# A graph network on one core: the two relational layers' dense loops and the second layer's tables in one block, with that layer's scale taken from a bound

## The chip, the cores and the metric

The kernel runs on 1 core of one Trainium2 chip. The metric is the device time of one execution in microseconds (us), and the median over several runs is compared. The core has five engines that run side by side and meet only at semaphores: TensorE (PE, matrix products), VectorE (DVE), ScalarE (ACT), GpSimd (POOL) and SyncE (SP, which here issues most of the DMAs).

## The reference, cut to what matters

A graph of 3125 nodes with 96 features and 103125 edges (source, destination, one of 8 relation types) goes through four residual steps, each followed by a layer norm: ten propagation steps, an attention over the edges, two relational layers, and two layers that sum over neighbours. The change is in the third step:

```
for l in range(2):                       # L2
    xb = h.reshape(N, B, S)              # 8 blocks of 12 features
    transformed = einsum('nbi,rbio->rnbo', xb, weights[l]).reshape(R, N, D)
    msg = transformed[etype, src] * (1 / in_degree)[dst]
    agg = segment_sum(msg, dst)
    h_new = agg + h @ loop_w[l] + bias[l]
    h = relu(h_new) if l == 0 else h_new
x = layernorm(x + h)
```

The input h of the first of the two layers is a layer norm's output; that of the second is the first's result through relu. weights[l] has 8 relations x 8 blocks x 12 x 12 values.

## The kernel before, in words

Nodes lie in NT = 25 tiles of 128. The kernel is a series of blocks. In a block each engine has its own written-out list of instructions; at a block's end all engines meet, and a block's PSUM tensors are freed and others allocated. The attention stage (main block from line 1263) comes first, then the relational layers (lines 1399 to 2050), then the last step (from 2060). For each relational layer (`for layer in range(2)`, line 1458) there are two blocks.

**Tables.** For each node tile t, PE multiplies the transposed features `ht` (97 rows, the last one all 1) with `bd`, the block-diagonal weights of all 8 relations beside loop_w and bias: one product of 480 columns and one of 384 into two PSUM banks, in f32 (`table_products`, L1494 and L1495). ACT takes loop_w's part into `hn` (L1499) and the relations' part, scaled to a safe power of two, as the f16 high half into `tab` (L1500, `high_out`). DVE writes the f16 low half, the scaled product less the high half (L1504, `low_out`). SP stores each tile of `tab` in memory (`store_table`, L1483). Three bank pairs are used in turn, so the product of tile t waits for the low half of tile t - 3.

**Dense loop.** For each of the TD = 19 first destination tiles and each of 8 relations DVE makes a mask of edge counts out of packed words in `code` (`relation_mask`, L1474; four mask buffers in turn, released by `s_free`), and PE adds 25 products mask x tab into one PSUM bank (`tile`, L1888). That is 3800 products per layer. The edges into the last GT = 6 tiles are done by gathering: ACT makes one-hot matrices (L1948 to L1956), POOL gathers 12 x 128 rows of the table from memory (L1864), each gather released by a tick of PE (`s_pace`), and PE multiplies them (L1896). Edges that the packed words can't hold go through `irregular_edges` (L1921, L1928) after tile 0. DVE reduces each finished bank (L1985) and adds it to `goal` (L1990), which is `hn` in the first layer and `x` in the second. At a loop's end DVE adds the last gathered tile and then the last dense tile.

**What sets the scale.** In the first layer, before any table, the scale is taken from `btop`: the weights' largest value times SUB = 12 times `LN_BOUND`, the largest value a layer norm of 96 features can give. `btop` comes from `bmost`, a [128, 2] tile that DVE fills in the attention stage (L1385, L1387) and POOL reduces over the partitions (L1282). In the second layer DVE takes the largest weight (L1509) and the largest value in all of `hn` (L1765). PE turns the two columns (L1748), DVE reduces them (L1514, L1515), PE spreads them over the partitions (L1751), and DVE works out the scale and the scaled degrees (L1768, L1769, L344 to L347, L1519 to L1521) and releases `s_sc`, for which PE waits before its first table product. The 25 transposes of `hn` (`rows_turned`, L1742), with ACT's relu copy of five at a time (L1782), stand around these steps.

The masks of the dense loop's first relations are made while the tables are made: four in the first layer, and in the second one ahead of DVE's low halves and one after each of the tiles 8, 14 and 20 (L1774 to L1776). SP loads the words of the first three tiles at the start of the block (L1723). The weights of the second layer are loaded into `bd` during the first layer's dense loop (`load_relations(e, 1, s_load)`).

Of the kernel before, what the change touches and what calls it, by code (L numbers as in the profile page):

```python
# [16 lines left out]
P = 128  # L17
N = 3125
D = 96
# [58 lines left out]
def gnn_kernel(nc, a, out):  # L78

    with ExitStack() as top:  # L80
# [1044 lines left out]
        bmost = sb("bmost", [P, 2], F32)  # L1125
        btop = sb("btop", [P, 2], F32)
# [3 lines left out]
        with ExitStack() as ph:  # L1130
# [115 lines left out]
            with ExitStack() as main:  # L1246
# [18 lines left out]
                with nc.Block() as block:  # L1265
                    @block.gpsimd
                    def _(e):
# [13 lines left out]
                        e.wait_ge(s_bd, 2)  # L1281
                        e.partition_all_reduce(btop[:], bmost[:], P, bass.bass_isa.ReduceOp.max).then_inc(s_bd, 1)  # L1282
                        e.wait_ge(s_bd, 3)
# [81 lines left out]
                    def _(e):  # L1365
# [33 lines left out]
        with ExitStack() as ph:  # L1399
            sb = new_sb(ph)  # L1400
            ht = flat
            most = sb("l2_most", [P, 2], F32)
            both = sb("both", [2, 3], F32)
            ones = sb("ones", [2, P], F32)
            st2 = sb("l2_maxima", [P, 2], F32)
# [52 lines left out]
            for layer in range(2):  # L1458
# [3 lines left out]
                s_in = [sem(nm + f"in{k}") for k in range(SLOTS)]  # L1462
                s_mask = sem(nm + "mask")

                def load_code(e, t):
                    e.dma_start(code[:, t % SLOTS, :, :, :].rearrange("p q s d -> p (q s d)"),
                                code_dram[t, :, :, :, :].rearrange("p q s d -> p (q s d)")).then_inc(s_in[t % SLOTS], 16)

                def relation_mask(e, t, r):

                    up = 10 - 2 * r
                    turned = mask[:, r % MR, :, :].rearrange("p s d -> p (s d)").bitcast(I32)
                    words = code[:, t % SLOTS, :, :, :].rearrange("p q s d -> p (q s d)").bitcast(I32)
                    e.tensor_scalar(turned.rearrange("p (s q d) -> p s q d", q=NQ, d=DQ // 2),  # L1474
                                    words.rearrange("p (q s d) -> p s q d", q=NQ, d=DQ // 2), abs(up), 0x0C000C00,
                                    ALU.logical_shift_left if up >= 0 else ALU.logical_shift_right,
                                    ALU.bitwise_and).then_inc(s_mask, 1)
# [11 lines left out]
                s_dve, s_most, s_mt, s_diag, s_mp, s_sc = (sem(nm + k) for k in ("tdve", "most", "most_t", "diag", "most_p", "sc"))  # L1489
# [16 lines left out]

                def weights_largest(e):
                    e.wait_ge(s_load, 16 * LOADS)
                    e.tensor_reduce(most[0:D, 0:1], bd[0:D, :, 0:HW2], mybir.AxisListType.XY, ALU.max,  # L1509
                                    apply_absolute_value=True).then_inc(s_most, 1)  # L1510

                def maxima_over_partitions(c, e, most_t):
                    e.wait_ge(s_mt, 1)
                    c(e.tensor_reduce(both[:, 0:1], most_t, AX_X, ALU.max))  # L1514
                    e.tensor_scalar(both[:, 1:3], ident[0:2, 0:2], both[:, 0:1], None, ALU.mult).then_inc(s_diag, 1)  # L1515
# [7 lines left out]
                if layer == 0:  # L1523
                    with ExitStack() as ph:
# [12 lines left out]
                        s_att, s_read, s_mean, s_sq, s_var, s_std, s_x, s_one = (  # L1537
                            sem("ln1_" + k) for k in ("att", "read", "mean", "sq", "var", "std", "x", "one"))
# [981 lines left out]
```

## Time and profile before

| | |
|---|---|
| median of 3 runs | 2339.51 us (2338.59 to 2343.16) |
| profiled execution, own time | 2347.8 us |
| its span, first to last instruction | 2346.1 us |
| PE / DVE / ACT / POOL busy in the span | 2155.6 / 1825.4 / 1164.0 / 881.5 us |
| mean granted TensorE clock | 0.965 |
| first layer's tables and dense loop | about 1369 to 1780 us |
| second layer's tables and dense loop | about 1782 to 2171 us |

The profile comes from one execution. Busy times are sums of an engine's instructions; the span is the time from the first to the last instruction, and what the execution took more than it lies around it. The granted clock is the share of full speed (2.4 GHz) that the chip grants TensorE; it is 1.00 or 0.50 at any moment, and a value between is a mean over a stretch.

### The profile page before, as it was taken

To read this page: it belongs to the slowest core of one execution; us is meant where nothing else is said; L and a number is where in the kernel's file an instruction comes from. 1 tells how busy PE (TensorE), PEld (TensorE's weight loads), DVE (VectorE), ACT (ScalarE), POOL (GpSimd) and SP (SyncE) were. 2 spreads that over 40 slices of the span, in tenths; PEclk is the share of its full clock that TensorE was granted. 3 is DMA by queue.
4 is the path that set the end of the run, shared out by engine and by line. 5 is a ranking of instruction groups with operands and counts; after the bars stand their busy time and mean duration, and the time that the engine had idled before them with its cause. 6 is when DMAs were issued, how large, how long until landed. Compare 5 with 4: busy or idle time off the path is not lost. (4 is left out here: it accounts for less than half of the span.)

```text
span 2346.1 us, 63182 instructions
## 1 busy us (share of the span) xinstructions
PE 2155.6 (92%) x22505; PEld 1791.3 (76%) x22505; DVE 1825.4 (78%) x2687; ACT 1164.0 (50%) x2788; POOL 881.5 (38%) x1062
## 2 busy tenths in 40 slices
PE   2888888899999999789999968999999999999897
PEld 2888887899999999522222235999996899999787
DVE  8999999655555666579999976988886788887446
ACT  1888888332332332379999955222313432230323
POOL 2444444000000000068888823555551455555000
PEclk8999999899999999789999979999999999999799
DMA  2444444210000010332222234232224323222800
GB/s 67 157 169 168 173 177 176 76 39 30 31 29 31 29 44 2 102 84 56 58 58 57 58 116 147 75 87 76 75 60 149 119 74 89 74 74 44 352 5 22
DMA packets 94801, 205.77 MB, mean 88 GB/s; under 512 B 21718, under 2 KB 61270, under 8 KB 94450
## 3 DMA queue, kind: packets, MB, share of 16 engines
q1 hardware_dynamic: 81458, 182.46, 22.3%
q0 software_dynamic: 13120, 20.18, 4.4%
q8 instruction: 159, 2.61, 0.5%
q14 instruction: 64, 0.52, 0.1%
HBM read 116.99 MB, written 84.76 MB: 86 GB/s over the span
## 5 line engine op out<-in xcount | busy, mean ns | idle before, releaser
L1888 PE MATMUL l_bank<-tab,mask 128*128 128x192 f16 x7600 | 636.8, 247 | 8.8 <-PEq L1719 3.5
L1888 PEld LDWEIGHTS l_bank<-tab,mask 128*128 128x128 f16 x7600 | 629.4, 98 | 11.9 <-issue 11.3
L1474 DVE TENSOR_SCALAR mask<-code 128x1600 int32<-128x1600 int32 x304 | 544.4, 1816 | 95.3 <-PE l_bank L1888 70.9
L1864 POOL DMA_INDIRECT ggot<-table_dram,gidx x408 | 386.8, 948 | 265.4 <-PE l_bank L1888 206.3
L1371 DVE TENSOR_TENSOR pr<-ex,count_copy 128x1568 f32<-128x1568 f32 x200 | 350.5, 1786 | 25.6 <-POOL ex L1270 13.8
L1361 ACT ACTIVATE ex<-score_pair,poss 128x784 f32<-128x784 f32 x400 | 344.2, 910 | 30.2 <-PE score_pair L1309 18.9
L1270 POOL TENSOR_SCALAR ex<-ex 128x1568 f32<-128x1568 f32 x200 | 298.5, 1493 | 78.5 <-ACT ex L1361 71.2
L906 PE MATMUL sums<-onehots,ct 128*128 128x192 f16 x3125 | 264.4, 248 | 11.2 <-issue 4.8
L906 PEld LDWEIGHTS sums<-onehots,ct 128*128 128x128 f16 x3125 | 261.5, 99 | 13.9 <-issue 7.5
L906 PE MATMUL sums<-u,ct 128*128 128x192 f16 x3125 | 259.1, 246 | 0.0
L906 PEld LDWEIGHTS sums<-u,ct 128*128 128x128 f16 x3125 | 258.0, 98 | 0.0
L459 POOL COPY wqk<-edges 128x6 f32 x400 | 163.7, 440 | 226.0 <-ACT wqk L643 113.3
L965 DVE TENSOR_REDUCE onehots<-sums 128x96 f32<-128x192 f32 x250 | 89.2, 357 | 176.2 <-PE sums L906 170.0
L1948 ACT ACTIVATE gidx<-rowidx 128x12 int32 x34 | 7.2, 211 | 428.0 <-PE l_bank L1896 387.4
L1309 PE MATMUL score_pair<-qa,ka 96*128 96x392 f16 x800 | 205.6, 340 | 3.6 <-ACT ex L1361 2.2
L1309 PEld LDWEIGHTS score_pair<-qa,ka 96*128 96x128 f16 x800 | 47.5, 98 | 184.8 <-ACT ex L1361 176.3
L1325 PE MATMUL att_acc<-pr,v 128*32 128x392 f32 x1600 | 176.5, 513 | 5.8 <-DVE pr L1371 5.8
L570 PE MATMUL counts<-onehots,flat 128*128 128x200 f16 x1200 | 143.1, 254 | 39.4 <-DVE onehots L491 35.5
L883 POOL PARTITION_ALL_REDUCE wtop<-wmax x1 | 0.4, 374 | 432.2 <-DVE wmax L996 432.2
L491 DVE TENSOR_TENSOR onehots<-iota,wqk 128x1200 f16<-128x1200 f16 x200 | 155.4, 777 | 0.0
L575 PE MATMUL codes<-onehots 128*128 128x200 f16 x1200 | 140.3, 251 | 0.0
L1042 ACT ACTIVATE u<-onehots,rdeg 128x96 f16<-128x96 f32 x125 | 46.7, 374 | 186.3 <-DVE onehots L965 186.2
(342 smaller groups left out, 2939.0 us busy)
## 6 DMA issues: line engine op xcount, KB each, us to landing
code<-code_dram SPq DMA_DIRECT2D x38, 800.0 KB
code_dram<-flat SPq DMA_DIRECT2D x100, 200.0 KB, 1.9
ct_dram<-ct SPq DMA_DIRECT2D x25, 800.0 KB, 3.6
c_dram<-flat SPq DMA_DIRECT2D x25, 800.0 KB, 3.4
ct_again<-ct_dram SPq DMA_DIRECT2D x25, 800.0 KB, 17.3
cring<-c_dram SPq DMA_DIRECT2D x200, 98.0 KB, 2.0
table_dram<-tab SPq DMA_DIRECT2D x50, 384.0 KB, 2.3
flat<-code_dram SPq DMA_DIRECT2D x19, 800.0 KB, 4.4
```

Source lines behind the costliest of these rows:

```text
L459: ins = e.tensor_copy(rec[:, w % RECS, h * GRP:(h + 1) * GRP, :], edge_rec[:, bass.ds(chunks[h], GRP), :])
L491: e.tensor_tensor(hot[:, k, :, :, :], iota[:], each(col[:, k, :], WC), ALU.is_equal).then_inc(s_hot, 1)
L570: e.matmul(counts[:, b, h * WC:(h + 1) * WC], chunk_of(srchot, k, j), chunk_of(hot, k, j), start=False, stop=False, skip_group_check=True)
L906: mm = e.matmul(sums[t % RS][:, 0:2 * D], ct[:, t, s, :], u[par][:, s, :, :].rearrange("p k d -> p (k d)"), start=(s == 0), stop=(s == NT ...
L1270: ins = e.tensor_scalar(ex[n % UR][:], ex[n % UR][:], EXP_HIGH, EXP_LOW, ALU.min, ALU.max)
L1309: mm = e.matmul(pair_ps[k][:, h, 0:QC], ka[0:D, k * HP2 + h, j * P:(j + 1) * P], qa[0:D, k * HP2 + h, b * QC:(b + 1) * QC], start=True, st ...
L1325: mm = e.matmul(acc[h * HW:(h + 1) * HW, b % 2, 0:QC], v[:, j, h, :], pr[n % UR][:, h, :], start=(j == 0), stop=(j == NT - 1), skip_group_ ...
L1361: e.activation(ex[n % UR][:, k * HP2:(k + 1) * HP2, :], pair_ps[k][:, :, 0:QC], ACT.Exp, scale=poss[:]).then_inc(s_ex[k], 1)
L1371: e.tensor_tensor(pr[n % UR][:], ex[n % UR][:], c_ps[n % 2][:, 0:QC].unsqueeze(1).to_broadcast([P, H, QC]), ALU.mult).then_inc(s_pr, 1)
L1474: e.tensor_scalar(turned.rearrange("p (s q d) -> p s q d", q=NQ, d=DQ // 2), words.rearrange("p (q s d) -> p s q d", q=NQ, d=DQ // 2), abs ...
L1864: e.indirect_dma_start(ggot[:, k, j, :], None, table_dram[:, :], bass.IndirectOffsetOnAxis(ap=gidx[:, k, j:j + 1], axis=0)).then_inc(s_ggo ...
L1888: mm = e.matmul(acc[k][:, 0:2 * D], mask[:, r % MR, s, :], tab[:, s, r, :], start=(r == 0 and s == 0), stop=(r == R - 1 and s == NT - 1))
```

## The change

One block now holds the first layer's dense loop, the second layer's tables and its dense loop (`stages`); the first layer's tables keep their block. One PSUM tensor `l2_bank` serves all three, and semaphores that both layers use (`s_in`, `s_mask`, `s_free`, `s_acc`, `s_gsum`) count on over the layers (`n = layer * TD + t`). The second layer's scale is worked out from a bound on the first layer's result: (the first layer's bound on the rows x 12 x the largest weight, plus (D + 1) times the largest of loop_w and bias) x 12 x the second layer's largest weight. For that the attention stage loads the second layer's weights once more and takes two more maxima.

```diff
-        bmost = sb("bmost", [P, 2], F32)
-        btop = sb("btop", [P, 2], F32)
+        bmost = sb("bmost", [P, 4], F32)
+        btop = sb("btop", [P, 4], F32)
+        W1_ROWS, W1_COLS = R * NB, SUB * SUB
+        w1_raw = spare[0:W1_ROWS, 4 * (HW2 + D):4 * (HW2 + D) + 2 * W1_COLS].bitcast(F32)
...  (attention stage, POOL: e.wait_ge(s_bd, 2) -> 4 and 3 -> 5 around partition_all_reduce)
...  (attention stage, SP)
                                 load_relations(e, 0, s_bd_in)
+                                e.dma_start(w1_raw, a["weights"][1].rearrange("r g i o -> (r g) (i o)")).then_inc(s_bd_in, 16)
...  (attention stage, DVE)
-                                e.wait_ge(s_bd_in, 16 * LOADS)
+                                e.wait_ge(s_bd_in, 16 * (LOADS + 1))
+                                e.tensor_reduce(bmost[0:D + 1, 2:3], bd[0:D + 1, 0, HW2:], AX_X, ALU.max,
+                                                apply_absolute_value=True).then_inc(s_bd, 1)
+                                e.tensor_reduce(bmost[0:W1_ROWS, 3:4], w1_raw, AX_X, ALU.max,
+                                                apply_absolute_value=True).then_inc(s_bd, 1)
...  (second layer's tables: weights_largest, maxima_over_partitions and what they use are gone)
+                def tables(bank):
+                    table = [bank[:, b:b + 2, :] for b in (6, 1, 4)]
+                    turned = [five(bank[:, b:b + 2, :]) for b in (4, 1)]
+                    def sync(e):
+                        for t in range(SLOTS):
+                            n = layer * TD + t
+                            e.wait_ge(s_mask, (n - SLOTS + 1) * R)
+                            load_code(e, n)
+                        for t in range(NT):
+                            e.wait_ge(s_lo, t + 1)
+                            store_table(e, t)
...  (gpsimd: the additions to x as before)
+                    def tensor(e):
+                        def rows_turned(g):
+                            if g == 0:
+                                e.wait_ge(s_acc, TD - 1)
+                            if g >= 2:
+                                e.wait_ge(s_ht, g - 1)
+                            e.wait_ge(s_goal, max(ADDED.index(t) + 1 for t in range(5 * g, 5 * g + 5)))
...  (five transposes)
+                        for g in range(G):
+                            rows_turned(g)
+                        e.wait_ge(s_load, 16 * LOADS)
+                        e.wait_ge(s_gsum, GT)
+                        for t in range(NT):
+                            e.wait_ge(s_ht, (1, 4, G)[t] if t < 3 else G)
+                            if t >= 3:
+                                e.wait_ge(s_lo, t - 2)
+                            table_products(e, table[t % 3], t)
+                    def vector(e):
+                        c = Chain(e, s_dve)
+                        c(e.tensor_scalar(power[:], btop[:, 2:3], float(D + 1), None, ALU.mult))
+                        c(e.tensor_scalar(scale[:], btop[:, 0:1], float(SUB) * LN_BOUND, None, ALU.mult))
+                        c(e.tensor_tensor(power[:], power[:], scale[:], ALU.add))
+                        c(e.tensor_scalar(power[:], power[:], btop[:, 3:4], float(SUB), ALU.mult, ALU.mult))
+                        degrees_scaled(c, e)
+                        e.wait_ge(s_free, layer * TD * R + MR)
+                        relation_mask(e, layer * TD, MR - 1)
+                        for t in range(NT):
+                            low_out(e, table[t % 3], t)
+                        e.wait_ge(s_xadd, G)
...  (scalar: as before)
...  (dense loop, PE)
                             for r in range(R):
+                                e.wait_ge(s_mask, n * R + (r + 1))
                                 for s in range(NT):
+                                    if layer and t == 0 and r == 0 and (s == 0 or s >= NT - 2):
+                                        e.wait_ge(s_lo, max(NT - 2, s + 1))
...  (dense loop, DVE: add_to_goal now releases s_goal; the loop's end)
+                        if layer == 0:
+                            code_there(e, TD)
+                            for r in range(MR - 1):
+                                masked(TD, r)
+                        summed(TD - 1)
                         for g, j in groups_behind(TD - 1) + groups_behind(TD):
                             if j == SLOTS - 1:
                                 gathered(g)
-                            summed(TD - 1)
...
+            main0 = layer_of(0)
+            tables1, main1 = layer_of(1)
+            with nc.psum_tensor("l2_bank", [P, 8, 512], F32) as l2_bank:
+                stages = [main0(l2_bank), tables1(l2_bank), main1(l2_bank)]
+                with nc.Block() as block:
...  (each engine runs its part of the three stages in turn)
```

`s_goal` counts the sums added to `goal`, and `ADDED` lists in which order they come, so that each group of five transposes waits only for its own tiles. In the words of before: `rows_turned(g)` stood in another block than the additions. Two memsets of POOL at the start of the first layer's tables (`most`, `ones`) are gone.

## Rows read from the trace of the kernel before

**Rows 1.** The page, engine totals, and its costliest group of DVE.

```profile
PE 2155.6 (92%) x22505; PEld 1791.3 (76%) x22505; DVE 1825.4 (78%) x2687; ACT 1164.0 (50%) x2788; POOL 881.5 (38%) x1062
...
L1474 DVE TENSOR_SCALAR mask<-code 128x1600 int32<-128x1600 int32 x304 | 544.4, 1816 | 95.3 <-PE l_bank L1888 70.9
```

**Rows 2.** Busy time by stretch: the second tables' start, the second dense loop.

```profile
core 0: us, PE busy (x) PEld busy (x) DVE busy (x) ACT busy (x) POOL busy (x), PEclk, DMA share, GB/s
...
1782.00:1800.00 18.00, 16.63 (x50) 9.66 (x50) 11.04 (x17) 8.23 (x15) 0.00 (x0) 0.72 0.50 192
...
1947.00:2160.00 213.00, 212.77 (x2579) 212.60 (x2578) 184.03 (x133) 52.51 (x138) 125.55 (x135) 1.00 0.27 71
```

**Rows 3.** Timeline: start, duration, engine, line, count, [idle before]; first loop to tables.

```profile
1777.78 1.15 PE L1896 MATMUL l_bank<-ggot,goh 128*128 128x192 f16 x12
1778.97 0.36 DVE L1985 TENSOR_REDUCE part<-l_bank 128x96 f32<-128x192 f32 x1 [6.97 <-PE l_bank L1896]
...
1779.99 0.32 DVE L1990 SCALAR_TENSOR_TENSOR hn<-part,rdk,hn 128x96 f32<-128x96 f32 x1
...
1781.84 3.41 PE L1742 MATMUL ht_bank<-ident,hn 128*96 128x128 f32 x15 [2.91 <-PEq L1834]
...
1785.29 0.70 ACT L1782 ACTIVATE flat<-ht_bank 96x640 f32<-96x640 f32 x1 [0.37 <-PE ht_bank L1742]
...
1786.91 0.21 DVE L1769 TENSOR_SCALAR tpower<-l_maxima 128x1 f32<-128x1 f32 x1
...
1788.26 0.17 DVE L1521 COPY rdk<-rds 128x6 f32<-128x6 f32 x1
...
1788.49 1.94 PE L1494 MATMUL ht_bank<-spare,flat 97*128 97x480 f32 x2 [1.14 <-DVE rdk L1521]
```

**Rows 4.** Timeline of the second tables: after a mask, and two undisturbed tiles.

```profile
1819.48 1.07 PE L1494 MATMUL ht_bank<-spare,flat 97*128 97x480 f32 x2 [0.48 <-DVE tab L1504]
...
1822.48 0.97 PE L1494 MATMUL ht_bank<-spare,flat 97*128 97x480 f32 x2
...
1823.93 0.97 PE L1494 MATMUL ht_bank<-spare,flat 97*128 97x480 f32 x2
```

**Rows 5.** Timeline: the second tables' end and the dense loop's start.

```profile
1829.84 0.81 PE L1495 MATMUL ht_bank<-spare,flat 97*128 97x384 f32 x2
...
1831.76 1.02 DVE L1504 SCALAR_TENSOR_TENSOR tab<-ht_bank,tscale,tab 128x768 f16<-128x768 f32 x1 [1.03 <-ACT tab L1500]
1831.87 1.19 POOL L1733 TENSOR_TENSOR x<-x,hn 128x480 f32<-128x480 f32 x1 [6.79 <-ACT tab L1500]
...
1834.11 11.13 PE L1888 MATMUL l_bank<-tab,mask 128*128 128x192 f16 x100 [3.46 <-PEq L1719]
...
1835.85 0.18 POOL L1851 COPY idx<-rowidx 128x1 int32 x1 [2.79 <-POOLq L362]
```

**Rows 6.** Stretches of PE alone: length, busy, granted clock, DMA share, GB/s.

```profile
1400.00:1409.00 9.00, 5.83 (x19) 1.00 0.37 151
...
1788.40:1795.00 6.60, 6.51 (x9) 0.51 0.17 69
1796.00:1830.70 34.70, 33.20 (x90) 1.00 0.59 238
1834.00:1840.00 6.00, 5.89 (x39) 0.52 0.17 57
```

**Rows 7.** Timeline of the first layer: five warm transposes; the dense loop's start.

```profile
1396.33 0.71 PE L1574 MATMUL ln_bank<-ident,x 128*96 128x128 f32 x5
...
1442.29 7.25 PE L1888 MATMUL l_bank<-tab,mask 128*128 128x192 f16 x86 [3.44 <-PEq L1539]
```

**Rows 8.** Timeline of the attention stage: weight loads, first maximum, POOL's reduction.

```profile
1049.62 0.27 SPq L356 DMA_DIRECT2D spare<-in_bias  x1
...
1051.91 0.51 PE L1317 MATMUL count_copy<-cring,exact 128*128 128x392 f16 x1 [7.32 <-DMA cring<-c_dram]
...
1142.65 0.94 DVE L1385 TENSOR_REDUCE bmost<-spare 96x1 f32<-96x768 f32 x1
...
1367.66 0.37 POOL L1282 PARTITION_ALL_REDUCE btop<-bmost  x1 [6.01 <-issue]
```

More of the change, by code:

```diff
@@ L1456, in gnn_kernel, with load_code @@
             s_load = sem("l2_load")
-            for layer in range(2):
+            s_in = [sem(f"l2_in{k}") for k in range(SLOTS)]
+            s_mask, s_free, s_acc, s_gsum, s_goal = (sem("l2_" + k) for k in ("mask", "free", "acc", "gsum", "goal"))
+            assert R % MR == 0
+            def load_code(e, n):
+                e.dma_start(code[:, n % SLOTS, :, :, :].rearrange("p q s d -> p (q s d)"),
+                            code_dram[n % TD, :, :, :, :].rearrange("p q s d -> p (q s d)")).then_inc(s_in[n % SLOTS], 16)
@@ new lines, in gnn_kernel @@
+            fixed = lambda g: SLOTS - 1 if g < GT - 1 else 1
+            GROUPS = [(g, k) for g in range(GT) for k in list(range(fixed(g))) + [SLOTS - 1]]
+            LAND = 60
+            DENSE = TD * R * NT
+            begun = [4 + i * (DENSE - LAND - 4) // (len(GROUPS) * GG) for i in range(len(GROUPS) * GG)]
+            ticks = {n - 1 - (n % NT == 0) for n in begun}
+            behind = [min(TD - 1, (begun[GG * n + GG - 1] + LAND - 1) // (R * NT)) for n in range(len(GROUPS))]
+            due = [sum(b <= t for b in behind) for t in range(TD)] + [len(GROUPS)]
@@ new lines, in gnn_kernel, with layer_of @@
+            assert len(ticks) == len(begun) < 1 << 16 and due[TD - 1] == len(GROUPS)
+            groups_behind = lambda t: GROUPS[due[t - 1] if t else 0:due[t]]
+            ADDED = [0]
+            for t in range(2, TD):
+                ADDED += [t - 1] + [g + TD for g, k in groups_behind(t - 1) if k == SLOTS - 1]
+            ADDED += [TD - 1] + [g + TD for g, k in groups_behind(TD - 1) + groups_behind(TD) if k == SLOTS - 1]
+            assert sorted(ADDED) == list(range(NT))
+            def layer_of(layer):
@@ new lines, in vector, with _ @@
+                        summed(TD - 1)
+                        for g, j in groups_behind(TD - 1) + groups_behind(TD):
+                            if j == SLOTS - 1:
+                                gathered(g)
+                    return sync, gpsimd, tensor, vector, scalar
+                return (tables, main) if layer else main
+            main0 = layer_of(0)
[3 more added lines that the diff above has]
+                with nc.Block() as block:
+                    @block.sync
+                    def _(e):
+                        for sync, _, _, _, _ in stages:
+                            sync(e)
+                    @block.gpsimd
+                    def _(e):
+                        for _, gpsimd, _, _, _ in stages:
+                            gpsimd(e)
+                    @block.tensor
+                    def _(e):
+                        for _, _, tensor, _, _ in stages:
+                            tensor(e)
+                    @block.vector
+                    def _(e):
+                        for _, _, _, vector, _ in stages:
+                            vector(e)
+                    @block.scalar
+                    def _(e):
+                        for _, _, _, _, scalar in stages:
+                            scalar(e)
```

515 lines of the change are left out of this document (214 added, 301 removed).

## The prediction

> **What bounds the kernel now.** I read the engine totals first: TensorE (PE) is busy for 92% of the span, far above VectorE (DVE) at 78%; the costliest group of DVE is the relation masks, 1.82 us each [rows 1]. That alone says nothing about this change, so the second view was the stage table. In the dense loop of the second relational layer PE is busy 212.77 of 213 us at full clock; in the stretch in which that layer's tables begin it has the granted clock 0.72 [rows 2]. So the loops are bound by PE, and what can be won lies at their borders. The third view, the timeline of the border, shows what stands there. The last product of layer 0 ends at 1778.93, DVE adds until 1780.31, the block ends, and PE starts again at 1781.84. Then come 25 transposes, with the search for the rows' maximum between them, and the scale chain, whose last instruction is at 1788.26. The first table product starts at 1788.49, 9.56 us after the last useful product [rows 3]. At the other end the last table product ends at 1830.65 and the first dense product starts at 1834.11: 3.46 us for ScalarE's (ACT's) copy, DVE's 1.02 us copy and a block border [rows 5]. The fourth view is the granted clock. It was 0.51 over the first 6.6 us of the tables and 0.52 over the first 6 us of the dense loop, both 1.2 GHz for nearly all of it, and 1.00 in between [rows 6].
>
> **Border one, loop 0 to tables.** Removed: the block border, the reduction over all of hn, the transposed maxima and their spreading product. PE's next instructions are the transposes. Groups 0 to 3 need sums that DVE has added by then, because the last dense tile's sum now goes before the gathered one, while PE still does its 12 gathered products (1.15 us). Five warm transposes took 0.71 us [rows 7] and ACT's copy of five takes 0.70 [rows 3]. With two buffers, counted from 1778.93: the first copy ends at 1.45 and frees group 2, which ends at 2.2; the second ends at 2.2 and frees group 3; the third ends at 2.95 and frees group 4, which ends at 3.65. The first product follows at once, since it needs only the first copy. 9.56 - 3.65 = 5.9 us saved. Bounds: nothing less than 25 transposes back to back (some 3.0 us), and if all ran cold, as those five did whose copy of 0.70 us came after 0.37 idle, 5 x 1.07, with the first wait some 5.5 us; so 4.1 to 6.6.
>
> The scale chain is no longer ahead of the products, only ahead of ACT's first copy. It has ten small operations; the seven from 1786.91 to 1788.43 took 1.5 us [rows 3], so ten take 2.1. They start when DVE's last addition ends, some 0.75 us after the last product, and end at 2.9 us. ACT's transposed copies end at 4.4 and the first table product at 5.1, so the chain costs nothing; without that cover it would cost its excess over 5.1. Behind it on DVE stands the fourth mask (1.82 us), over at 4.8, before DVE's first table copy can start at 6.2. The other three masks move into layer 0's last dense tile, into DVE's 6.97 us without work [rows 3]. They take 5.5 us; each waits for a mask buffer that PE frees every 2.05 us (25 products of 82 ns), and the last is over just before PE is. If they overran, the tile's sum would come late by that much, and group 3 of the transposes has 2.2 us to spare.
>
> **The tables.** Now 1788.49 to 1830.65 = 42.16 us. A warm tile takes 1.45 us (1822.48 to 1823.93), so 25 take 36.25. The rest is two things: half clock at the start, and three masks of 1.8 us between DVE's copies, after which PE waited for a buffer (0.48 us idle, and a tile 0.75 us longer) [rows 4, 6]. 3 x 0.75 = 2.2; the clock has the other 3.6. The change moves the masks away, and if PE stays warm through the transposes the clock's part goes too: 5.9 us, bounds 2.2 (clock falls again) to 5.9. Late next would be ACT: 0.90 and part of 0.25 us for each tile, 1.04 against 1.45, so PE remains the bound.
>
> **Border two, tables to loop 1.** The dense loop now waits for DVE's copy number 22, and its last two products of the first relation for copies 23 and 24. A copy ends 2.13 us after its product (1830.65 to 1832.78) [rows 5], so copy 22 ends 0.8 us before the last product does. Copy 24 ends 2.13 after; 24 dense products take 2.0. 3.46 - 0.2 = 3.2 us saved, bounds 1.3 (the loop waits for copy 24) to 3.4. The first 100 dense products took 11.13 us [rows 5]; in layer 0, where the clock had not fallen although the pause before was as long, 86 took 7.25 [rows 7], so 100 take 8.43. Saved: 2.7, bounds 0 and 2.8, since the same pause has cost nothing once.
>
> Waits added here: DVE waits for GpSimd's (POOL's) last addition to x, over 2.4 us after the last product [rows 5]; behind it stands the mask that needs relation 0 finished, at 2.3 us; nothing is lost, as PE wants it at 8.4. The gathers still need all tables in memory: POOL's first index copy came 3.07 us after DVE's last copy [rows 5], now 5.2 us into the loop instead of 1.7. The 3.5 us of delay fall into a first tile of 16.5 us, at whose end their first data are used. On SP the three code loads go ahead of the table stores; their masks' condition is met at 1772, so nothing queues behind them.
>
> **End of loop 1.** The last sum of 0.36 us and its addition of 0.32 [rows 3] go under the gathered products: 0.7 us saved.
>
> **Costs in the attention stage.** SP issues one more load of weights in the place where PE already waits 7.32 us for counts queued behind such loads; an issue takes 0.27 [rows 8]: 0.3 us, bounds 0 and 0.6. DVE does two more reductions, over 96 and 144 elements where 768 took 0.94 us [rows 8]: by size 0.3, with a start 0.45, bounds 0 and 1.9. ACT and DVE are both nearly full here, so I take 0.3. The reduction over partitions gets four columns for two, and POOL ends this block last: it took 0.37 with 6.01 us of issue ahead [rows 8]; nearest is nothing to 0.37, I take 0.1, and 6.4 if all of it grew with the columns.
>
> **Sum.** 5.9 + 5.9 + 3.2 + 2.7 + 0.7 - 0.7 = 17.7 us. The profiled execution took 2347.8 us (span 2346.1 and 1.7 around it), so 2330.1. It was 0.35% above the median, 2339.51, from which the same sum gives 2321.8; I say 2322.
>
> **Rivals.** (1) The clock falls in the transposes or the first tables. For it: it fell there before, when PE transposed with pauses, and after the pause in which the scale was awaited. Against: in layer 0's tables it stayed 1.00 over 9 us in which PE was busy 5.83 [rows 6], and transposes and tables now are denser than that. Price: a fall cost 3.6 us at the tables: 2325.5. The Trainium skill speaks for this rival ("TensorE: Matmul & The Clock Gate", A second HAM failure mode): PE that idles briefly but often while it cycles through PSUM banks has its clock go down and up again. By it the saving would lack that same fall; the 9 us at 1.00 disagree with it, the 0.51 agrees.
>
> (2) The change does only part of what it says: a wait returns at a border (copy 24 before the loop, 2.1 us, with it a cold start, 2.7), or the attention costs are at their upper ends (8.9 for 0.7). 5 to 9 us less: 2327 to 2331; with both, 2335, no change.
>
> (3) Slower. The two dense loops and the tables become one stretch of some 710 us in which PE never rests. If the granted clock falls inside it, each microsecond at half speed costs half a microsecond: it takes 45 us at 1.2 GHz to turn 17.7 us gained into 4.7 lost, 2344 and more. For it: nothing so long is in the trace. Against: 213 us at 1.00 with PE busy throughout [rows 2].
>
> **How the numbers follow.** Forecast 55%, own range 2318.5 to 2324.5; rival 1 22%; rival 2 17%, of which 6% end within 0.2%; rival 3 6%. A measurement of this kernel tells about 0.2%, 4.7 us, from no change. So faster 0.88, same 0.06, slower 0.06. The range goes from 2317 to 2331, with rival 1 and most of rival 2 in it.
>
> **What would show it.** Right: PE idle under 1 us between layer 0's last gathered product and the first transpose; first table product 3.4 to 4.2 us after it; table products 1.45 us apart from the first on, with clock 1.00; less than 0.4 us between the last table product and the first dense one; the first 100 dense products in about 8.4 us; a pause near 7.6 us at the counts in the attention stage. Wrong: a clock of 0.5 in any of these stretches, table tiles at 2.9 us, PE waiting in loop 1 for gathered rows after the first tiles, or POOL's reduction ending more than 0.5 us later after the last clip than before.

## The result, and the profile after

The changed kernel takes 2327.55 us (median of 4 runs, 2326.39 to 2328.19), the kernel before 2341.34 beside it (4 runs, 2338.59 to 2344.73). The ratio is 0.994, with a 95% interval of 0.9926 to 0.9954: 13.8 us less, between 10.8 and 17.3. I had said 2322. The time is 5.5 us above that: 1.8 of them lie in the kernel before, whose median was 2339.51 when I took it and 2341.34 beside the changed one, and 3.9 in the saving, 13.8 us for 17.7. It lies outside the 2318.5 to 2324.5 that I had put on the forecast and where I had put rival 2, and yet neither condition of that rival came: between the two loops every stretch became what the forecast said.

The page of after, engine totals and DVE's costliest group, against [rows 1]:

```profile
PE 2143.6 (92%) x22502; PEld 1784.1 (77%) x22502; DVE 1827.9 (79%) x2687; ACT 1164.4 (50%) x2788; POOL 884.8 (38%) x1060
...
L1477 DVE TENSOR_SCALAR mask<-code 128x1600 int32<-128x1600 int32 x304 | 548.7, 1817 | 81.4 <-PE l_bank L1876 80.4
```

PE has the same work but for three small products, and its busy time is 12.0 us shorter, of 21.0 between the two spans: over half of that difference is nearly the same work done in less time, with the mean granted clock at 0.972 for 0.965. The totals show no more. The timeline of after at border one (start, duration, engine, line, [idle before]) answers [rows 3]:

```profile
1774.56 1.15 PE L1884 MATMUL l_bank<-ggot,goh 128*128 128x192 f16 x12
...
1775.55 1.26 PE L1752 MATMUL l_bank<-ident,hn 128*96 128x128 f32 x10
...
1777.05 1.35 PE L1752 MATMUL l_bank<-ident,hn 128*96 128x128 f32 x10 [0.24 <-ACT flat L1781]
...
1778.30 0.17 DVE L1536 COPY rdk<-rds 128x6 f32<-128x6 f32 x1
1778.38 1.81 DVE L1477 TENSOR_SCALAR mask<-code 128x1600 int32<-128x1600 int32 x1
...
1778.59 0.75 PE L1752 MATMUL l_bank<-ident,hn 128*96 128x128 f32 x5 [0.19 <-ACT flat L1781]
...
1779.18 0.97 PE L1519 MATMUL l_bank<-spare,flat 97*128 97x480 f32 x2
...
1780.63 0.97 PE L1519 MATMUL l_bank<-spare,flat 97*128 97x480 f32 x2
```

The last gathered product ends at 1775.71 and the first table product starts at 1779.18, 3.47 us later, 9.56 before. The transposes wait only for ACT's copies, 0.24 and 0.19 us. The scale chain ends at 1778.47, long before ACT's first table copy, and the fourth mask runs behind it. The tables are 1.45 us apart from the first on.

Busy time of PE by stretch in after, against [rows 2, 6]: length, busy, granted clock, DMA share, GB/s.

```profile
1775.00:1779.00 4.00, 3.56 (x33) 1.00 0.00 0
1779.00:1785.00 6.00, 6.00 (x21) 1.00 0.17 66
1785.00:1816.00 31.00, 31.00 (x92) 1.00 0.69 271
1816.00:1822.00 6.00, 5.79 (x71) 1.00 0.46 178
...
1830.00:2150.00 320.00, 318.73 (x3877) 1.00 0.28 71
```

The clock is 2.4 GHz (1.00) in all of them; nowhere between the two loops does it fall. So the rival that it falls in the transposes or tables did not come, nor the one that it falls in the long stretch without rest. The Trainium skill ("TensorE: Matmul & The Clock Gate", A second HAM failure mode) has the clock go down and up where PE idles briefly and often between groups of products; the two pauses of 0.24 and 0.19 us here did nothing of the kind.

The timeline of after at border two, against [rows 5]:

```profile
1814.79 0.81 PE L1520 MATMUL l_bank<-spare,flat 97*128 97x384 f32 x2
...
1815.43 2.15 PE L1876 MATMUL l_bank<-tab,mask 128*128 128x192 f16 x24
...
1816.71 1.02 DVE L1529 SCALAR_TENSOR_TENSOR tab<-l_bank,tscale,tab 128x768 f16<-128x768 f32 x1 [0.43 <-ACT tab L1525]
...
1817.79 8.42 PE L1876 MATMUL l_bank<-tab,mask 128*128 128x192 f16 x100 [0.21 <-DVE tab L1529]
...
1820.86 0.18 POOL L1836 COPY idx<-rowidx 128x1 int32 x1 [2.84 <-POOLq L362]
```

The dense loop starts as the last table product ends, its 24 products cover DVE's last copy but for 0.21 us, and 100 more take 8.42 us, where I had said 8.43. POOL's first index copy is 5.4 us into the loop, and PE waits for nothing in its first 124 products but those 0.21 us.

The end of loop 1 in after, against the sums in [rows 3] and the term of 0.7 us:

```profile
2147.58 1.15 PE L1884 MATMUL l_bank<-ggot,goh 128*128 128x192 f16 x12
...
2149.16 0.32 DVE L1978 SCALAR_TENSOR_TENSOR x<-part,rdk,x 128x96 f32<-128x96 f32 x1
2152.60 0.26 POOL L2172 MEMSET early<- 97x192 f32 x1 [10.16 <-POOLq L94]
2152.68 0.06 DVE L2393 MEMSET umax<- 128x1 f32 x1 [3.19 <-PEq L94]
```

DVE is done at 2149.48, but the next stage starts 3.1 us later. Before, DVE was done 3.0 us ahead of it too, and POOL had been idle for 10.70 us. This idle time of POOL's queue (POOLq) belongs to none of my steps; what it is comes below.

The attention stage of after, against [rows 8]:

```profile
1049.17 0.55 SPq L1296 DMA_DIRECT2D spare<-in_weights  x1
...
1052.01 0.51 PE L1320 MATMUL count_copy<-cring,exact 128*128 128x392 f16 x1 [8.18 <-DMA cring<-c_dram]
...
1142.87 0.25 DVE L1388 TENSOR_REDUCE bmost<-spare 97x1 f32<-97x96 f32 x1
1143.03 0.28 DVE L1390 TENSOR_REDUCE bmost<-spare 64x1 f32<-64x144 f32 x1
1143.24 0.93 DVE L1392 TENSOR_REDUCE bmost<-spare 96x1 f32<-96x768 f32 x1
...
1368.16 0.39 POOL L1284 PARTITION_ALL_REDUCE btop<-bmost  x1 [5.87 <-issue]
```

The new load's issue takes 0.55 us and PE's wait for counts grew by 0.86, from 7.32; the two new reductions push the old one back by 0.37 us (1142.87 to 1143.24); the reduction over partitions grew by 0.02. The stage ends only 0.5 us later, but that is not its price: in this execution PE came to the wait 0.76 us earlier than in that of before. The wait is 7.32 and 7.33 us in the two profiles without the load and 8.12 to 8.26 in the twelve with it, so the load costs 0.8 to 0.9 us. From DVE's first reduction to the next stage's first product it is 226.4 and 226.5 us in those two and 226.7 to 227.1 in the ten others in which this border is unchanged, which agrees with 0.37 for the reductions. Together that is 1.2 us.

### The profile page after: what moved, and what is told of

It is laid out like the page before. It is cut to its first block and busy times, and to the rows that moved or that the text cites. A ratio compares the mean times of both kernels' runs of the same rounds, so it can differ in the third digit from the quotient of the medians.

```text
span 2325.1 us, 63183 instructions
## 1 busy us (share of the span) xinstructions
PE 2143.6 (92%) x22502; PEld 1784.1 (77%) x22502; DVE 1827.9 (79%) x2687; ACT 1164.4 (50%) x2788; POOL 884.8 (38%) x1060
## 3 DMA queue, kind: packets, MB, share of 16 engines
q8 instruction: 159, 2.61, 0.4%
```

## Experiments

The milestones below are differences between rows of the timeline of each kernel's one profiled execution: (a) the last product of loop 0 to the first transpose, (b) from there to the first table product, (c) the tables, (d) the last table product to loop 1, (e) the first 100 dense products. Negative means that the modelled ends overlap.

```
                 time us   ratio to before [95%]     (a)    (b)    (c)    (d)    (e)
before, rows 3-6 2341.34                             2.91   6.65  42.16   3.46  11.13
before_again     2342.39   1.0003 [0.9993, 1.0014]   2.89   7.63  40.69   3.46  10.07
after            2327.55   0.9940 [0.9926, 0.9954]  -0.16   3.63  36.41  -0.16   8.79
border_one       2331.45   0.9959 [0.9946, 0.9971]   3.04   4.65  36.63  -0.16   8.79
border_two       2340.16   0.9995 [0.9985, 1.0004]  -0.16   3.63  36.42  12.35  10.09
three            2336.05   0.9975 [0.9965, 0.9984]   3.04   4.72  36.56   3.43  10.06
drain_early      2340.51   0.9995 [0.9986, 1.0004]  -0.16   3.63  36.42  12.15  10.26
drain_first      2329.94   0.9956 [0.9944, 0.9969]  -0.16   3.63  36.42   3.43  11.16
masks_back       2329.36   0.9942 [0.9928, 0.9955]  -0.16   3.63  38.86  -0.16   8.79
maxima           2333.89   0.9962 [0.9949, 0.9976]  -0.16   7.67  39.58  -0.16   8.79
```

**The kernel before once more** (before_again), for how far its executions differ.

> The kernel before, unchanged, for a second profile. The two profiled executions differ by 21.0 us in span, the medians by 13.8. Theory A (the profiled execution of before was untypical): its dense loop of layer 0 had pauses of PE by issue between 1449 and 1464 us that cost 3.7 us, and a cold start of loop 1; a second profile lacks the pauses (layer 0's loop 333 us and not 336.6) and perhaps the cold start (first 100 dense products in 8.4 us and not 11.1), with a span of 2338 to 2343. Theory B (the pauses belong to the kernel and the change removed them): the second profile has them again, with a span near 2346.

Its 12 runs go from 2338.34 to 2347.25, 9 us apart; the 4 of after lie within 1.8. Its profile shows the same borders with other costs: the tables 40.69 us for 42.16, loop 1's first 100 products 10.07 for 11.13. The clock of PE in two stretches of this second profile, at the tables' start and at loop 1's, answers [rows 6], which had 0.51 and 0.52:

```profile
1786.00:1792.00 6.00, 5.12 (x10) 0.53 0.25 106
1834.00:1840.00 6.00, 6.00 (x63) 0.83 0.14 30
```

So a pause of one and the same length (3.46 us) is followed now by one, now by another stretch at half clock. A term read from one execution is one draw of it. Of the two theories A came true for the pauses. In the first profile loop 0 has pauses of PE, 2.4 us in all between 1449.5 and 1463.9, at full clock; the second has none there:

```profile
1441.00:1451.00 10.00, 7.74 (x88) 1.00 0.31 83
1451.00:1465.00 14.00, 12.61 (x160) 1.00 0.30 90
```

```profile
1451.00:1465.00 14.00, 14.00 (x185) 1.00 0.30 88
```

The cold start of loop 1 came again, but smaller, and the span, 2342.4 us, is in theory A's range.

**Border one back** (border_one), **border two back** (border_two), **both back** (three), with everything else as changed:

```diff
-                with nc.Block() as block:
+                for chunk in (stages[0:1], stages[1:3]):     # border_two: [0:2], [2:3]; three: [0:1], [1:2], [2:3]
+                    with nc.Block() as block:
```

> The changed kernel with the block border back between layer 0's dense loop and the second layer's tables (the words of tile 19 are loaded in the loop). Bound, masks and the open second border stay. My theory: PE starts its transposes 2.4 us later, and the clock falls in the pause, which costs 1 to 2 us in the transposes and 3.6 at the tables: against the changed kernel 2.4 us more if the clock holds, 6 to 8 if it falls. Rival: the maximum search was the whole cost of this border, and the border itself costs under 1 us.

> The changed kernel with the block border back between the second layer's tables and its dense loop. My theory: 3.5 us of border, and a cold start of 2.7 in those executions in which the clock falls: 3.5 to 6.2 us more than the changed kernel. Rival: ACT's and DVE's copies of the last tile were the price of this place and a border costs next to nothing: under 2.5 us.

> The changed kernel with both borders back: what is left of the change is the bound in place of the rows' maximum, and the moved masks. If the two borders' costs add: the sum of the two runs above, 6 to 14 us more than the changed kernel. Against the kernel before it should still be faster by the maximum search and the masks: 3.5 + 2.2 us and the 0.7 us of the loop's end, less 0.7 in the attention stage, 5.7 us. If the clock falls here in any case (rival), the clock's part of the tables is not won and the borders seem cheaper one at a time than together.

Border one costs 3.9 us, 3.2 in (a) and 1.0 in (b). That is between my two cases: the clock fell to 0.50 from 1780.8 to 1784.2, in the transposes, and was back at 1.00 as the tables began. Border two cost 12.6 us, twice the most that I had expected. And both together cost 8.5, less than border two alone. No sum of two border prices gives that: something is paid once, cheaply at border one and dearly at border two. The rows of border_two at border two:

```profile
1827.27 6.95 PE L1876 MATMUL l_bank<-tab,mask 128*128 128x192 f16 x62 [12.35 <-PEq L2055]
1827.38 0.18 POOL L1836 COPY idx<-rowidx 128x1 int32 x1 [10.05 <-POOLq L362]
```

The table copies end at 1817.06 and POOL's addition at 1817.33; then all five engines are idle. The trace's records of the engines' own sequencers, which the views above leave out, name it: GpSimd executes a DRAIN, an instruction that stands at every block end.

```
GpSimd's DRAIN at block ends (start + us), gathers since the last one?
              border one             border two             end of loop 1
before        1771.60 + 9.96 (yes)   1833.27 + 0.04 (no)    2162.82 + 9.94 (yes)
after                                                       2141.41 + 9.94 (yes)
border_one    1768.73 + 9.94 (yes)                          2146.18 + 9.93 (yes)
border_two                           1817.54 + 8.89 (yes)   2154.54 + 9.93 (yes)
three         1771.73 + 9.94 (yes)   1825.98 + 0.04 (no)    2154.03 + 9.93 (yes)
```

The drain takes 9 to 10 us where GpSimd has issued indirect gathers since the last one, even 49 us after the last gather, and 0.04 us where it has not. How many gathers there were makes no difference: 410 led up to that of after, 205 to each of the two in before. It explains [rows 3] too: PE's 2.91 us between 1778.93 and 1781.84, which I had put down to DVE's sums (done at 1780.31) and a block's end, ended 0.28 us after the drain did, at 1781.56; the other engines' drains there had ended by 1780.34. The Trainium skill ("Perfetto Trace Analysis", Sequencer-only Instruction) says that such a record begins only when all its semaphores are satisfied. The trace agrees: border_two's starts 0.21 us after the last addition's end, so its 8.89 us are the drain's own. Right behind a gather the record is longer because it begins some 0.1 us before that gather's own instruction does. In all 21 long drains of the fourteen profiles the end comes 8.9 us after the last gather's instruction has ended, or after the drain's own start where that is later. What GpSimd does in these 8.9 us no run shows. It is not a wait for gathered rows on their way, which PE had used 42 us before border_two's drain began.

**The drain paid elsewhere** (drain_early, drain_first): border_two, with GpSimd drained inside the tables block; each kernel has one of the two additions.

```diff
                         for g in range(G):
                             e.wait_ge(s_hi, 5 * g + 5)
                             e.tensor_tensor(x[:, tiles(g), :], x[:, tiles(g), :], hn[:, tiles(g), :], ALU.add).then_inc(s_xadd, 1)
                             e.wait_ge(s_xadd, g + 1)
+                            if g == 0:            # drain_first
+                                e.drain()
+                        e.drain()                 # drain_early
```

> The kernel with the block border back between the tables and loop 1, as in border_two (12.6 us behind the changed kernel, PE idle 12.35 us at that border), and GpSimd drained once inside the tables block, right after its last addition to x, where GpSimd has nothing else to do. Theory (the 12 us are GpSimd's drain, which takes some 10 us the first time after the indirect gathers of loop 0, wherever it is asked for): the drain now lies under the 36 us of tables, the border's own drain takes well under 1 us, PE idles 3.4 us at the border as in the kernel before, and with a start of loop 1 at half clock (1.3 us) the time is 4 to 5 us behind the changed kernel, 2332. Rival (a border there waits for something else, such as the table stores to land, or any border costs what it costs): 12.35 us of idle again and 2340. Second rival (GpSimd's part is an end of a block as such, not its drain): 12 us again with the explicit drain short.

This one missed: 12.15 us of idle and 2340.51. My edit was at fault, not the theory: the last addition of the five comes at the tables' end, so the drain stood where the border's stood. It did rule one rival out: the explicit drain took the 8.89 us (from 1818.06) and the block's own then 0.03, so it is the drain and not the end of a block. Drawn earlier:

> As drain_early (block border back between tables and loop 1), but GpSimd is drained after its first of five additions to x in the tables block, at about 1789, 26 us before the border. In drain_early the drain stood behind the last addition, whose place is the end of the tables, so it was no earlier than the border's own: PE idled 12.15 us all the same, and the explicit drain had the 8.89 us while the border's was short. Theory (the 10 us are the first drain after the indirect gathers, and are paid once, wherever asked for): the drain ends at about 1799 under the tables, the border's own is short though four additions lie between, PE idles 3.4 us, and the time is 4 to 5 us behind the changed kernel, 2332. Rival (any GpSimd work after a drain makes the next one long, so only a drain with nothing behind it helps): 12 us again, 2340.

POOL's timeline in drain_first, and PE's at border two:

```profile
1788.57 1.20 POOL L1741 TENSOR_TENSOR x<-x,hn 128x480 f32<-128x480 f32 x1 [18.34 <-ACT tab L1525]
1798.78 1.20 POOL L1741 TENSOR_TENSOR x<-x,hn 128x480 f32<-128x480 f32 x1 [9.01 <-ACT tab L1525]
...
1821.63 0.18 POOL L1838 COPY idx<-rowidx 128x1 int32 x1 [2.81 <-POOLq L362]
```

```profile
1819.84 12.40 PE L1878 MATMUL l_bank<-tab,mask 128*128 128x192 f16 x115 [3.43 <-PEq L2057]
```

The drain (1789.80 + 8.88) lies under the tables, the border's own takes 0.04 us though four additions came between, PE is idle 3.43 us as in [rows 5], and 2340.16 has become 2329.94. That shows the theory, and rules out a wait for the table stores, which this kernel has as well: an instruction added took 10 us out.

**The gathers 30 products earlier** (earlier_gathers), so that the drain at loop 1's end starts sooner.

```diff
-            LAND = 60
+            LAND = 90
```

> The changed kernel with each gather asked for 90 dense products before it is due instead of 60, so the last gather of a loop starts some 30 x 82 ns = 2.46 us earlier. Nothing else moves. Theory (the end of loop 1 is set by GpSimd's drain, 9.94 us from its last gather, at 2151.35 against DVE's last addition at 2149.48): the drain then ends 2.4 us earlier and DVE sets the end, 1.8 us less between the last product of loop 1 and the next stage; 1.8 us faster than the changed kernel, 2325.7. Rival (the end waits for DVE's sums, as I had read it when I predicted): no difference, 2327.5. Loop 0's end has no border and gains nothing by either.

2325.93 us, ratio 0.9925 [0.9912, 0.9939]. The end of loop 1 in this kernel:

```profile
2150.13 0.32 DVE L1978 SCALAR_TENSOR_TENSOR x<-part,rdk,x 128x96 f32<-128x96 f32 x1
2151.76 0.26 POOL L2172 MEMSET early<- 97x192 f32 x1 [10.82 <-POOLq L94]
```

From DVE's last addition to the next stage it is 1.31 us, 3.12 in after; from loop 1's last product to the next stage's first 5.93, 7.66 in after. 1.73 of the 1.8 foretold: the stage behind loop 1 had waited for the drain. Here it ends at 2149.84, ahead of DVE's last addition (2150.45). The two intervals of the ratios overlap, so the time alone would not show it; the rows do.

**The masks back between the table copies** (masks_back).

```diff
                         for t in range(NT):
                             low_out(e, table[t % 3], t)
+                            if t in (8, 14, 20):
+                                relation_mask(e, layer * TD, (t - 2) // 6)
```

> The changed kernel with three of the four masks put back between DVE's table copies (after tiles 8, 14 and 20), as before; one block still. By my term of the sum: each makes its tile 0.75 us longer, tables 2.2 us longer (36.4 to 38.6) with the clock still at 1.00, 2329.8. Rival (the fall of the clock came from the pauses that these masks made): the clock falls in the tables as well, 3.6 us more, 2333. Second rival (the masks were hidden, and all that the tables lost was clock): 2327.5.

The tables take 38.86 us, 2.45 more, with the clock at 1.00 throughout; 2329.36 us. PE's row behind the first of the masks, as in [rows 4]:

```profile
1796.25 1.04 PE L1519 MATMUL l_bank<-spare,flat 97*128 97x480 f32 x2 [0.58 <-DVE tab L1529]
```

**The scale from the rows' maxima, in the one block** (maxima): of the change, only the bound is taken back, and the attention stage keeps its load and reductions.

```diff
-                        c(e.tensor_scalar(power[:], btop[:, 2:3], float(D + 1), None, ALU.mult))
...
+                        e.tensor_reduce(most[:, 1:2], hn[:], mybir.AxisListType.XY, ALU.max).then_inc(s_most, 1)
...
+                        e.matmul(most_p, ones[:], both[:, 1:3], start=True, stop=True).then_inc(s_mp, 1)
```

> The changed kernel with the scale taken again from the maximum over the rows of hn, inside the one block: two reductions on DVE, a transpose and a spreading product on PE between the transposes, and PE's first table product waits for the scale. If the border was only the block (theory of the rival: the bound brings nothing once the block is gone): first table product within 1 us of the changed kernel's 3.47 us, 2328. By my steps: DVE's last addition ends 0.75 us after the last product, the two reductions, the transposed maxima and the scale chain follow, the product comes some 4.2 us later than in the changed kernel, 2331.7 if the clock holds, up to 2335 if the wait makes it fall for the first tables.

2333.89 us, 6.3 behind the changed kernel. Its timeline:

```profile
1778.04 2.64 DVE L1788 TENSOR_REDUCE l_most<-hn 128x1 f32<-128x2400 f32 x1
...
1784.02 1.94 PE L1523 MATMUL l_bank<-spare,flat 97*128 97x480 f32 x2 [1.33 <-DVE rdk L1540]
```

and the stretch behind it (length, busy, clock):

```profile
1784.00:1790.00 6.00, 5.98 (x9) 0.50 0.00 0
1790.00:1824.00 34.00, 34.00 (x100) 1.00 0.64 259
```

The product comes 4.04 us later (I had said 4.2), and with PE's pauses of 2.13 and 1.33 us ahead of it the clock is at 1.2 GHz for 6 us and the tables take 3.17 longer. I had priced such a fall at 3.6. In border_one and three, with the bound and the block border, the tables ran at 1.00 (36.63 and 36.56 us); in both profiles of before and in maxima, without the bound, they began at half clock. So it is the bound that keeps the clock up in the tables, as far as one profile of each variant tells.

**Three more cuts**, to see what the readings are worth. reduce_later moves POOL's reduction over partitions from the attention block's end to the next block, with DVE's first use of it later there; all_one puts the first layer's tables into the same block; best is both with the gathers 30 products earlier.

```diff
-                        e.wait_ge(s_bd, 4)
-                        e.partition_all_reduce(btop[:], bmost[:], P, bass.bass_isa.ReduceOp.max).then_inc(s_bd, 1)
...
+                                e.partition_all_reduce(btop[:], bmost[:], P, bass.bass_isa.ReduceOp.max).then_inc(s_top, 1)
...
-                stages = [main0(l2_bank), tables1(l2_bank), main1(l2_bank)]
+                stages = [tables0(l2_bank), main0(l2_bank), tables1(l2_bank), main1(l2_bank)]
```

> The changed kernel with GpSimd's reduction over partitions of the attention stage moved from the end of its block to the start of the next one, where DVE needs its result only for the scale of the first layer, now computed behind four of the five groups of sums. Theory (the attention block ends with the reduction, 1368.55 against DVE's last copy of sums at 1365.72, with 5.9 us of issue ahead of 0.39 of work): the next stage's transposes start 2.8 us earlier and 2.8 us are gained, 2324.7. Rival (the 5.9 us of issue come with the reduction and now stand in front of DVE's scale, or GpSimd's part is hidden anyway): 0, 2327.5.

> The changed kernel with the first layer's tables merged into the same block as well, by the same means (dense loop 0 waits for DVE's copy 22, its last products of the first relation for copies 23 and 24). Theory (border three is like border two): PE idle between the first layer's last table product and dense product 3.53 us before, -0.16 after, so 3.7 less; the constants that GpSimd then makes beside loop 0 cost up to 0.4: 3.3 us faster than the changed kernel, 2324.2, clock 1.00 through the border. Rival (loop 0's first products wait for its first mask or code words, loaded in the tables block, or for the constants): 1 us or nothing, 2326.5 or more.

> The changed kernel with the first layer's tables in the block, the reduction over partitions moved into the tables block, and gathers asked for 90 products ahead. If the three gains lie at three different places of TensorE's path they add: 3.3 + 2.8 + 1.7 = 7.8, 2319.7 and 22 us faster than the kernel before. If a start at half clock moves to another place, or a merged first block waits for the reduction, 3 us less: 2322.7.

reduce_later 2323.43 us, 0.9927 [0.9914, 0.994]; all_one 2323.40, 0.9926 [0.9913, 0.9939]; best 2318.94 (4 runs, 2318.69 to 2319.64), 0.9908 [0.9893, 0.9922]: 22 us under the kernel before, 8.6 under the changed one, where 7.8 was foretold. Singly the two gave 4.1 and 4.2 us by the medians; the rows below show 3.0 and 3.6 of them, and the intervals hold both. The 6 runs of reduce_later spread over 7.1 us, so the borders taken out are not all that makes executions differ. The first row shows reduce_later's first transposes, at 1369.68 in after; the second all_one's first dense product, with no idle ahead:

```profile
1366.68 0.74 PE L1574 MATMUL ln_bank<-ident,flat 128*128 128x128 f32 x5 [1.59 <-PEq L94]
```

```profile
1440.62 5.58 PE L1872 MATMUL l_bank<-tab,mask 128*128 128x192 f16 x62
```

## Why the prediction was right, and short by 4 us

The three main places (the two borders and the tables) gave what I had said, by the steps that I had said, but for the drain at border one. The end of loop 1 gave its 0.5 us by another step, and the costs were larger. Each term with what the first profile of before, its second one, and after show:

```
                        said   first - after        second - after
border one              5.9    9.56 - 3.47 = 6.1    10.52 - 3.47 = 7.1
tables                  5.9    42.16 - 36.41 = 5.8  40.69 - 36.41 = 4.3
border two              3.2    3.62 - 0.36 = 3.3    3.3
loop 1's cold start     2.7    11.13 - 8.43 = 2.7   10.07 - 8.43 = 1.6
end of loop 1           0.7    4.49 - 3.95 = 0.5    0.5
attention, costs       -0.7    -0.86 - 0.37 = -1.2  -1.2
sum                     17.7   17.2                 15.6
```

(Border two: 3.46 + 0.16, less the 0.36 by which after's first 100 products, 8.79 with DVE's wait, exceed 8.43.)

**Border one.** Right in size: 3.65 said, 3.47 measured. Wrong in a cause: I had PE's 2.91 us wait for DVE's sums and the block, and it was for GpSimd's drain. The change gains from it all the same, since there is no block end any more at which to drain. With the block gone the bound is worth 4.04 us here (maxima); with the bound there the block is worth 4.2, (a) and (b) of border_one. They overlap: the sum of the two is more than what both together gave.

**Tables.** Right: 2.2 for the masks (2.45 in masks_back), the rest clock. That rest was 3.6 in the first profile and 1.8 in the second (4.3 less 2.45).

**Border two.** Right, because in the kernel before border one had paid the drain, so that this border cost its 3.46 us and no more. Had the change merged only loop 0 and the tables, it would have gained 1.2 us, which the interval does not tell from nothing, and not 14 (border_two). That both borders went together was luck as far as my reasons go. My list of rivals had no such case.

**Loop 1's cold start.** The mechanism is right, 8.42 us for 100 warm products. The size was one draw: 2.7, 1.6 the next time, and in the ten milestones above 8.79 wherever there was no pause and 10.06 to 11.16 where there was one (3.43 to 12.35 us).

**End of loop 1.** The step failed. Taking a last sum out from behind the products moved DVE's end, but the block waited for the drain: it ends 2.61 us after loop 1's last product in before and in after alike, and earlier_gathers shows that the next stage waits for it. The 0.5 us came behind the drain. From its end to DVE's first instruction of the next stage it was 1.87 us and is 1.34, and the sequencer's records put most of that on GpSimd's clearing of the semaphores (0.59 and 0.33 us behind it, then 0.52 and 0.03). That clearing stood in none of my terms.

**Costs in attention.** The load cost more than my bound: the issue on SP was 0.55 us for 0.27, and the wait grew by 0.86 where I had 0.3, at most 0.6. The reductions cost 0.37 for 0.3, the one over partitions 0.02 for 0.1. In sum 1.2 for 0.7.

**The 3.9 us that are missing** of 17.7 (13.8 measured, and its interval, 10.8 to 17.3, would let 0.4 to 6.9 be missing). Against the execution that I took the terms from they fall short by 0.5 only, the cost in attention. But that execution (2347.8) is 6.4 us above its kernel's median, 2341.4, and above every timed run of before, while after's own (2327.12) is 0.4 below its. The weak step is "from which the same sum gives": I went from the execution to the median and left the terms as they stood, though two of them, 3.6 and 2.7 for the clock, are of the kind by which executions differ. With the second profile they are 1.8 and 1.6, border one is 1.0 more, and the sum is 15.6, inside the measured interval. That is argued from two profiles and not shown. The 1.8 us between it and 13.8 are less than the measurement tells, and stay open.

Stretches that I had no term for differ by as much. The last stages, from the next stage's first product, take 168.7 us in after for 167.6 and 167.8 in the two profiles of before, and 167.1 to 170.0 in the eleven variants, though none of them changes anything there. Loop 0 goes the other way: 336.65 and 335.35 us before, 334.57 in seven variants and 332.92 in after. In the first that is the pauses of PE shown above, at full clock; in the second it is the clock, 0.70 in its first 10 us

```profile
1441.00:1451.00 10.00, 9.14 (x82) 0.70 0.27 69
```

for 1.00 in after, behind the same pause of 3.44 to 3.53 us. Nor is it all the clock: each run's mean granted clock is on record, and among 15 runs of before the fastest and the slowest (2336.65 and 2345.42 us) have the same 0.966. Which pauses a median execution of before takes cold stays open: only profiled ones have rows.

## What to carry to other kernels

Before pricing a block border, read what each engine still has to do there, its sequencer's own instructions too: idle time with a queue as its releaser (POOLq, 10.70 us at loop 1's end) was in the profile of before. At border one no view names it, and only the sequencer's record shows the drain; the engine that held that border was not the one with the last visible instruction. A term that stands for a clock fall belongs in the sum with its mean over executions, which here takes a second profile; the terms of waits, read once, came out to 0.2 us (3.65 and 3.47 us at border one, 3.2 and 3.3 at border two). And take borders out together or test them alone: two borders that share one cost have no price each.

## What the hardware showed that I had not expected

The first drain of GpSimd after its indirect gathers ends 8.9 us after the last gather's instruction, and takes the same 8.9 us where that gather lies 20 or 49 us back; right behind a gather its record reads 9.94, 1.04 of which lie under the gather. The next drain takes 0.04 us. An explicit drain in GpSimd's idle time takes the cost off the path: 10.2 us here.

The same pause of PE, 3.43 to 3.53 us, was followed at the start of a dense loop by a clock of 0.52, 0.70, 0.83 or 1.00 over some 6 to 10 us. In maxima it fell to 0.50 in a stretch with two shorter pauses of 2.13 and 1.33 us, with transposes between them; behind two pauses of 0.24 and 0.19 us it stayed at 1.00 (after).
